# Layer 0's probabilities transposed by DMA, their product with V two steps later, and the queues reordered around it

## The chip, the cores and the metric

The kernel runs on one NeuronCore of a Trainium2 chip. A core has TensorE (PE in the profile, its weight loads as PEld), VectorE (DVE), ScalarE (ACT), GpSimd (POOL), SyncE (SP), which here only issues DMAs, and 16 DMA engines. The metric is the time of one execution on the device in microseconds (us). Each engine runs its own list of instructions in order; they wait for one another through semaphores.

## The reference

Two graph-attention layers over 128 graphs of 128 nodes with 512 channels. What layer 0 computes per graph, with 8 heads of 64 channels:

```python
h = relu(layernorm(x))
m = h @ map_w.T + map_b
n = m_heads / max(norm(m_heads), 1e-8)
cos_adj = ((n @ n.T) * ~mask > 0.1)
q, k = m @ q_w.T + q_b, m @ k_w.T + k_b        # folded into weights that act on h
p = softmax(where(mask, -1e10, q @ k.T / 8))
a = cos_adj * p
x = x + relu((a @ v @ gcn_W.T) / (a.sum(-1) + 1))    # v = h @ gcn_map_w.T + b, gcn_W folded in
```

Layer 1 is a plain masked attention with 4 heads and an output projection on the result. The change leaves it alone.

## The kernel before

Layer 0 takes the graphs in 32 groups of four (QUAD) and walks over 256 **steps**, n = 8 t + u: step u of group t handles graph u // 2 of the group and one half (HB = 4) of its 8 heads. Matrices that need more precision than f16 are split into an f16 high part and an f16 rest, and each product is three f16 matmuls per 128 rows of depth (line 161).

The order of each engine's work is written out by hand in one `group(t)` per engine, without a planner. In step u of group t TensorE runs, in this order: a projection of the next group (m for u < 4, q for u >= 4; 12 matmuls), `prob_transpose(n)` (four f32 transposes through the identity, from `cprobs` in SBUF into the PSUM bank `ps_pt`, line 836), `scores(n + 1)` (8 f32 matmuls of q and k at line 821, 12 f16 matmuls of n with n at line 828, all into the one pair of banks `ps_sc`), a second projection (v or k), and `weigh_values(n)` (12 matmuls of 66 columns into `ps_av`, line 848). So a step needs results of its own step: the transposes wait for `select_similar(n)` on VectorE, `weigh_values(n)` waits for `cpT_low(n)`.

The loop through the other engines is: `row_max` (VectorE, four instructions with mask and row maximum, line 119), `exps` (ScalarE, four exponentials with their sums, line 504), `select_similar` (VectorE, line 620, gives `cprobs`), the transposes on TensorE, `cpT_high` (ScalarE, line 511: PSUM to f16), `cpT_low` (VectorE, line 626: the f16 rest), `row_max` of the next step. `probs` and `cprobs` have one buffer each. After `weigh_values` VectorE runs `epilogue(n)` (three instructions, lines 636 to 644), GpSimd adds the residual (line 422), and SP stores the graph (line 325) and loads the next residual (line 321).

Beside it the next groups are prepared: `stats` (VectorE, lines 84 and 86; all four graphs of a group in step 7), `factors` (GpSimd), `relu` and `h_high` (ScalarE, lines 464 and 470), `h_low` (VectorE, line 582), `transpose_h` (SP, a DMA transpose of 128 x 1024 f16 into `hT`, line 311); and for n: `m_copy` (VectorE, line 587), `square` (ScalarE, line 485), `head_sums` (VectorE), `head_norms` (15 chained GpSimd instructions for each graph) and `normalise` (GpSimd), `n_high` (ScalarE, line 490), `n_low` (VectorE, line 604), `transpose_n` (SP, the same size, line 317). A projection waits until the one before it in its PSUM bank has been copied out (`m_copy`, `v_copy`, `q_copy` line 474, `k_copy` line 479). SP issues every DMA of the kernel from one queue, in program order, waits included; x comes by one DMA of 1 MB for each group.

## Time and profile before

| what | value |
|---|---|
| median of three runs | 2928.79 us (2925.0 to 2929.02) |
| the profiled execution's own time | 2929.56 us |
| its span, first to last instruction | 2927.2 us |
| mean granted TensorE clock | 0.98 |
| busy over the span: PE, DVE, ACT, POOL | 96%, 67%, 59%, 52% |
| DMA moved | 318.36 MB, 109 GB/s on average |

The profile is of one execution. Busy shares are means over stages with different limits: layer 0 runs up to about 1960 us, layer 1 from there on. The end of a matmul is modelled, so the distance from one group's start to the next group's start is what says how long a piece of TensorE's work takes.

### The profile page before, as it was taken

What the parts mean: (1) busy time and instruction counts of PE and PEld (TensorE: products, weight loads), DVE (VectorE), ACT (ScalarE), POOL (GpSimd) and SP (SyncE); (2) the same over time, 40 slices, a digit from 0 to 9 for tenths busy, and PEclk for the clock granted to TensorE, in tenths of its full rate; (3) what the DMA queues carried; (4) which work ended last, traced back from release to release, by engine and by line L of the source; (5) the groups of instructions that cost most, each with busy time, mean ns of one, the idle gap of its engine ahead of it and who ended that gap; (6) DMA issues with size and microseconds to landing.
All of it is one profiled execution on the core that took longest, in us unless ns stands there. A gap on an engine that the chain in (4) does not pass through costs nothing. (4 is left out here: it accounts for less than half of the span.)

```text
span 2927.2 us, 65410 instructions
## 1 busy us (share of the span) xinstructions
PE 2796.1 (96%) x21910; PEld 1596.1 (55%) x21910; DVE 1950.6 (67%) x6356; ACT 1724.5 (59%) x4891; POOL 1531.0 (52%) x4146
## 2 busy tenths in 40 slices
PE   5999999999999999999999999948999999999997
PEld 2455555555555555555555555534555555555554
DVE  4576677667666766676676667656667676666764
ACT  3466556656655665566566556545666666666663
POOL 1565556556645665565566456513455554555441
PEclk8999999999999999999999999969999999999998
DMA  4244334533443443344333434335565555655652
GB/s 128 52 88 110 89 83 94 110 82 88 98 100 82 88 109 97 81 92 114 82 88 96 103 82 88 80 102 123 142 159 153 154 149 144 162 148 157 151 132 65
DMA packets 555741, 318.36 MB, mean 109 GB/s; under 512 B 452496, under 2 KB 454032, under 8 KB 555408
## 3 DMA queue, kind: packets, MB, share of 16 engines
q1 hardware_dynamic: 555408, 314.19, 44.4%
q8 instruction: 176, 2.88, 0.4%
q14 instruction: 157, 1.29, 0.1%
HBM read 146.32 MB, written 67.11 MB: 73 GB/s over the span
## 5 line engine op out<-in xcount | busy, mean ns | idle before, releaser
L504 ACT ACTIVATE probs<-probs,negmax 128x128 f32<-128x128 f32 x1024 | 398.2, 390 | 423.6 <-DVE negmax L119 423.6
L422 POOL TENSOR_TENSOR o_sb<-o_sb,xres 128x512 f32<-128x512 f32 x128 | 162.7, 1271 | 434.6 <-DVE o_sb L644 434.6
L626 DVE SCALAR_TENSOR_TENSOR cpT_lo<-ps_pt,cpT_hi 128x512 f16<-128x512 f32 x256 | 176.7, 690 | 296.3 <-ACT cpT_hi L511 296.3
L161 PE MATMUL ps_pj<-wm_hi,hT 128*128 128x512 f16 x1024 | 326.5, 380 | 15.0 <-DVE wm_lo L669 15.0
L161 PE MATMUL ps_pj<-wv_hi,hT 128*128 128x512 f16 x1024 | 326.8, 380 | 0.0
L161 PE MATMUL ps_pj<-hT,wk_hi 128*128 128x512 f16 x1024 | 305.8, 380 | 0.0
L161 PE MATMUL ps_pj<-hT,wq_hi 128*128 128x512 f16 x1024 | 304.5, 379 | 0.0
L511 ACT ACTIVATE cpT_hi<-ps_pt 128x512 f16<-128x512 f32 x256 | 151.5, 592 | 256.3 <-PE ps_pt L836 256.3
L1102 ACT ACTIVATE l_probs<-l_probs,l_negmax 128x128 f32<-128x128 f32 x512 | 199.1, 390 | 150.2 <-DVE l_negmax L119 150.2
L1071 POOL TENSOR_TENSOR l_xres<-l_xres,l_bo_rows 128x512 f32<-128x512 f32 x128 | 172.9, 1351 | 150.9 <-DMA l_xres<-x_scratch 150.9
L119 DVE CUSTOM_DVE_ANT_0 probs<-ps_sc,mask 128x128 f32<-128x128 f32 x1024 | 233.9, 284 | 3.6 <-PE ps_sc L828 3.6
L836 PE MATMUL ps_pt<-ident,cprobs 128*128 128x128 f32 x1024 | 158.3, 278 | 52.7 <-DVE cprobs L620 52.7
L161 PE MATMUL ps_pj<-wm_lo,hT 128*128 128x512 f16 x512 | 194.7, 380 | 0.0
L161 PE MATMUL ps_pj<-wv_lo,hT 128*128 128x512 f16 x512 | 194.0, 379 | 0.0
L161 PE MATMUL ps_pj<-hT,wq_lo 128*128 128x512 f16 x512 | 194.0, 379 | 0.0
L161 PE MATMUL ps_pj<-hT,wk_lo 128*128 128x512 f16 x512 | 194.0, 379 | 0.0
L620 DVE SCALAR_TENSOR_TENSOR cprobs<-ps_sc,bound,probs 128x512 f32<-128x512 f32 x256 | 189.8, 742 | 4.9 <-ACT probs L504 4.5
L504 ACT ACTIVATION_READ_ACCUMULATOR probs<-probs,negmax 128x1 f32 x1024 | 191.0, 187 | 0.0
L161 PE MATMUL l_ps_pj<-l_wv_hi,l_hT 128*128 128x256 f16 x1024 | 189.8, 274 | 0.0
L836 PEld LDWEIGHTS ps_pt<-ident,cprobs 128*128 128x128 f32 x1024 | 126.5, 143 | 111.2 <-DVE cprobs L620 69.2
L821 PE MATMUL ps_sc<-room 64*128 64x128 f32 x2048 | 186.0, 301 | 0.0
L84 DVE BATCH_NORM_STATS2 ln_st<-xg 128x6 f32<-128x512 f32 x256 | 173.1, 676 | 15.2 <-DMA xg<-in_x 14.9
(196 smaller groups left out, 7204.1 us busy)
## 6 DMA issues: line engine op xcount, KB each, us to landing
xg<-in_x SPq DMA_DIRECT2D x32, 1024.0 KB, 5.6
xres<-in_x SPq DMA_DIRECT2D x128, 256.0 KB, 2.9
x_scratch<-o_sb SPq DMA_DIRECT2D x128, 256.0 KB, 2.1
xg<-x_scratch SPq DMA_DIRECT2D x128, 256.0 KB, 3.0
l_xres<-x_scratch SPq DMA_DIRECT2D x128, 256.0 KB, 3.4
out<-l_o_sb SPq DMA_DIRECT2D x128, 256.0 KB, 3.7
mask_u<-in_adj SPq DMA_DIRECT2D x32, 64.0 KB, 2.8
hT<-h SPq DMA_TRANSPOSE x128, 3.2
```

The source lines that it names most:

```text
L84: nc.vector.bn_stats(st[:, 0:6], x).then_inc(bn_done, 1)
L119: last = nc.vector.tensor_tensor_reduce(masked[:, i], scores[:, i // 2, (i % 2) * P:(i % 2 + 1) * P], mask, -1.0, FLOAT_MAX, ALU.add, ALU. ...
L161: last = pe.matmul(out, a(kt), b(kt), start=(n == 0), stop=(n == 3 * kts - 1))
L422: nc.gpsimd.tensor_tensor(o_sb[:, j % 2], o_sb[:, j % 2], xres[:, j % 2], ALU.add).then_inc(res_done, 1)
L504: last = nc.scalar.activation(probs[:, i], probs[:, i], ACT.Exp, bias=negmax[:, u % 2, i:i + 1], scale=-1.0, accum_out=zsum[:, u % 4, hh:h ...
L511: nc.scalar.activation(cpT_hi[:], ps_pt[:].rearrange("p (h n) -> p h n", h=HB), ACT.Copy, scale=F16_SCALE).then_inc(cph_done, 1)
L620: nc.vector.scalar_tensor_tensor(cprobs[:].rearrange("p (b h) n -> p b (h n)", b=2), ps_c, bound[:, t % 2, j:j + 1], probs[:].rearrange("p ...
L626: nc.vector.scalar_tensor_tensor(cpT_lo[:], ps_pt[:].rearrange("p (h n) -> p h n", h=HB), F16_SCALE, cpT_hi[:], ALU.mult, ALU.subtract).th ...
L821: nc.tensor.matmul(ps_s[:, b, pl * P:(pl + 1) * P], q_sb[rows, t % 2, pr, cols], k_sb[rows, t % 2, pr, cols], start=True, stop=True)
L836: mm = nc.tensor.transpose(ps_pt[:, hh * P:(hh + 1) * P], cprobs[:, hh], ident[:])
L1071: nc.gpsimd.tensor_tensor(xres[:, n % 2], xres[:, n % 2], bo_rows[:], ALU.add).then_inc(res_ready, 1)
L1102: last = nc.scalar.activation(probs[:, hh], probs[:, hh], ACT.Exp, bias=negmax[:, n % 2, hh:hh + 1], scale=-1.0, accum_out=zsum[:, n % 2, ...
```

## The change

- `prob_transpose`, `ps_pt`, `cpT_high` and `cpT_low` go. `p_high` (ScalarE) and `p_low` (VectorE) split `cprobs` where it lies, in SBUF, into `c16` (two buffers of 128 x 1024 f16, both parts), and SP transposes that by DMA into `cpT` (four buffers): one `transpose_p(n)` in each step.
- `weigh_values(n - 2)` and `epilogue(n - 2)` run in step n; the last two steps' follow after the loop. The freed PSUM banks give `ps_sc` and `ps_av` a second buffer each, so `scores(n)` waits for step n - 2 of the readers and no longer for n - 1. The banks of the weights' norms are shared with these.
- x is loaded graph by graph (256 KB each, waiting only for its own graph's `relu`), and `stats` of a group are spread: one graph in steps 5 and 6, two in step 7, all behind the epilogue.
- GpSimd's `head_norms` treats two graphs in one chain of 15 instructions on twice the width, in steps 2 and 4; `n_high`, `n_low` and `transpose_n` come one step later.
- In SP's list the store and the residual load stand behind the step's transposes, and for the graph whose last half was finished by the epilogue of the step before. `add_residual` moves back by one graph accordingly.
- `stage["v"]`, used in the weights' preparation alone, takes the place of half of `hT`.

The core of the diff (changes of names in the preparation are left out):

```diff
-stage["v"] = sb("stage_v", [P, KT, D])[:]
+hT = sb("hT", [P, 2, 2 * KT, QUAD * P], F16)
+stage["v"] = hT[:, 1].rearrange("p k n -> p (k n)").bitcast(F32).rearrange("p (k n) -> p k n", k=KT)
...
-hT = sb("hT", [P, 2, 2 * KT, QUAD * P], F16)
...
-norm_st = sb("norm_st", [P, 2, 4, H0])
-consts = sb("consts", [P, 4, H0])
+norm_st = sb("norm_st", [P, 4, QUAD, H0])
+consts = sb("consts", [P, 4, 2 * H0])
...
-cpT_hi = sb("cpT_hi", [P, HB, P], F16)
-cpT_lo = sb("cpT_lo", [P, HB, P], F16)
+c16 = sb("c16", [P, 2, 2, HB, P], F16)
+cpT = sb("cpT", [P, 4, 2 * HB, P], F16)
...
-ps_sc = ctx.enter_context(nc.psum_tensor("ps_sc", [P, 2, 512], F32))
-ps_s, ps_c = ps_sc[:, :, 0:2 * P], ps_sc[:, :, 2 * P:]
-ps_pt, ps_av = bank("ps_pt"), bank("ps_av")
+ps_sc = [ctx.enter_context(nc.psum_tensor(f"ps_sc{n}", [P, 2, 512], F32)) for n in range(2)]
+ps_s = [both[:, :, 0:2 * P] for both in ps_sc]
+ps_c = [both[:, :, 2 * P:] for both in ps_sc]
+ps_av = [bank("ps_av0"), bank("ps_av1")]
...
-const_loaded, x_loaded = sem("const_loaded"), sem("x_loaded")
+ps_norm = [ps_av[1][:], ps_sc[1][:, 0], ps_sc[1][:, 1], ps_av[0][:]]
+const_loaded = sem("const_loaded")
+x_loaded = [sem(f"x_loaded{j}") for j in range(QUAD)]
...
-pj_ready, s_ready, pt_ready, av_ready = pe_sems = [
-    sem(n) for n in ("pj_ready", "s_ready", "pt_ready", "av_ready")]
+cpT_loaded = [sem(f"cpT_loaded{n}") for n in range(2)]
+pj_ready, s_ready, av_ready = pe_sems = [sem(n) for n in ("pj_ready", "s_ready", "av_ready")]
...
     def load_weight(dst, src, loaded):
...
-    sp.dma_start(xg[:], xt[0]).then_inc(x_loaded, 16)
+    def load_graph(g, j):
+        if g:
+            sp.wait_ge(relu_done, count(QUAD * (g - 1) + j + 1))
+        sp.dma_start(xg[:, j], xrt[g, j]).then_inc(x_loaded[j], 16)
+    for j in range(QUAD):
+        load_graph(0, j)
...
+    def transpose_p(n):
+        sp.wait_ge(cpl_done, count(n + 1))
+        if n >= 4:
+            sp.wait_ge(av_ready, count(n - 3))
+        sp.dma_start_transpose(cpT[:, n % 4], c16[:, n % 2].rearrange("p s h n -> p (s h n)")).then_inc(
+            cpT_loaded[n % 2], 16)
     def load_residual(t, j):
...
-    def load_graphs(g):
-        sp.wait_ge(relu_done, count(QUAD * g))
-        sp.dma_start(xg[:], xt[g]).then_inc(x_loaded, 16)
...
-    sp.dma_start(xg[:], xt[1]).then_inc(x_loaded, 16)
+    for j in range(QUAD):
+        load_graph(1, j)
...
-    load_graphs(2)
+        load_graph(2, j)
...
     def group(t):
...
-            if u % 2 == 0 and t + u:
-                i = QUAD * t + u // 2
-                store(*divmod(i - 1, QUAD))
-                if i + 1 < B:
-                    load_residual(*divmod(i + 1, QUAD))
...
-            if proj and 3 <= u < 3 + QUAD:
-                transpose_n(t + 1, u - 3)
+            if proj and 4 <= u:
+                transpose_n(t + 1, u - 4)
...
-            if t + 3 < GROUPS and u == 6:
-                load_graphs(t + 3)
+            transpose_p(8 * t + u)
+            i = QUAD * t + u // 2 - 2
+            if u % 2 == 0 and i >= 0:
+                store(*divmod(i, QUAD))
+                load_residual(*divmod(i + 2, QUAD))
+            if t + 3 < GROUPS and 3 <= u < 3 + QUAD:
+                load_graph(t + 3, u - 3)
...
+    store(GROUPS - 1, QUAD - 2)
...
     def head_norms(g, j):
...
-        pool.wait_ge(sum_done, count(QUAD * g + j + 1))
-        n2, r, a, vh = (norm_st[:, j % 2, n] for n in range(4))
-        link = chained(pool, norm_chain, count(NORM_OPS * (QUAD * g + j)), NORM_OPS)
+        pool.wait_ge(sum_done, count(QUAD * g + j + 2))
+        n2, r, a, vh = (norm_st[:, n, j:j + 2] for n in range(4))
+        minus_half, three_halves = (consts[:, n].rearrange("p (j h) -> p j h", j=2) for n in range(2))
+        link = chained(pool, norm_chain, count(NORM_OPS * (2 * g + j // 2)), NORM_OPS)
...
-        rsqrt_steps(nc, link, r, n2, vh, a, consts[:, 0], consts[:, 1])
+        rsqrt_steps(nc, link, r, n2, vh, a, minus_half, three_halves)
...
     def normalise(g, j):
...
-        pool.wait_ge(norm_chain, count(NORM_OPS * (QUAD * g + j + 1)))
-        nc.gpsimd.tensor_tensor(heads, heads, norm_st[:, j % 2, 1].unsqueeze(2).to_broadcast([P, H0, DH]),
+        pool.wait_ge(norm_chain, count(NORM_OPS * (2 * g + j // 2 + 1)))
+        nc.gpsimd.tensor_tensor(heads, heads, norm_st[:, 1, j].unsqueeze(2).to_broadcast([P, H0, DH]),
...
     def v_low(g, j):
...
-        normalise(0, j)
+        if j % 2:
...
+            normalise(0, j - 1)
+            normalise(0, j)
...
     def group(t):
...
-                head_norms(t + 1, u - 1)
+            if proj and u in (2, 4):
+                head_norms(t + 1, u - 2)
+                normalise(t + 1, u - 2)
...
-            if u % 2:
-                add_residual(t, u // 2)
+            i = QUAD * t + (u - 3) // 2
+            if u % 2 and i >= 0:
+                add_residual(*divmod(i, QUAD))
...
+    add_residual(GROUPS - 1, QUAD - 1)
...
 def _(act):
...
-    def cpT_high(n):
-        act.wait_ge(pt_ready, count(n + 1))
-        act.wait_ge(av_ready, count(n))
-        nc.scalar.activation(cpT_hi[:], ps_pt[:].rearrange("p (h n) -> p h n", h=HB), ACT.Copy,
-                             scale=F16_SCALE).then_inc(cph_done, 1)
+    def p_high(n):
+        act.wait_ge(cp_done, count(n + 1))
+        act.wait_ge(cpT_loaded[n % 2], 16 * (n // 2))
+        nc.scalar.activation(c16[:, n % 2, 0], cprobs[:], ACT.Copy, scale=F16_SCALE).then_inc(cph_done, 1)
...
     def weight_high(n, kind):
...
+            p_high(n)
...
-            cpT_high(n)
...
-            if proj and 2 <= u < 2 + QUAD:
-                n_high(t + 1, u - 2)
+            if proj and 3 <= u < 3 + QUAD:
+                n_high(t + 1, u - 3)
...
     def stats(g, j):
-        dve.wait_ge(x_loaded, 16 * (g + 1))
+        dve.wait_ge(x_loaded[j], 16 * (g + 1))
...
     def head_sums(g, j):
...
-        dve.wait_ge(n_done, count(QUAD * g + j - 1))
-        nc.vector.tensor_reduce(norm_st[:, j % 2, 0], sq[:].rearrange("p (h c) -> p h c", h=H0), AX_X,
+        if g:
+            dve.wait_ge(n_done, count(QUAD * (g - 1) + j + 1))
+        nc.vector.tensor_reduce(norm_st[:, 0, j], sq[:].rearrange("p (h c) -> p h c", h=H0), AX_X,
...
     def n_low(g, j):
...
-        mask_scores(nc, dve, s_ready, count(n + 1), probs, ps_s, mask[:, t % 2, u // 2],
+        mask_scores(nc, dve, s_ready, count(n + 1), probs, ps_s[n % 2], mask[:, t % 2, u // 2],
...
     def select_similar(n):
...
-        dve.wait_ge(pt_ready, count(n))
-        nc.vector.scalar_tensor_tensor(cprobs[:].rearrange("p (b h) n -> p b (h n)", b=2), ps_c,
+        nc.vector.scalar_tensor_tensor(cprobs[:].rearrange("p (b h) n -> p b (h n)", b=2), ps_c[n % 2],
...
-    def cpT_low(n):
+    def p_low(n):
...
-        nc.vector.scalar_tensor_tensor(cpT_lo[:], ps_pt[:].rearrange("p (h n) -> p h n", h=HB), F16_SCALE,
-                                       cpT_hi[:], ALU.mult, ALU.subtract).then_inc(cpl_done, 1)
+        nc.vector.scalar_tensor_tensor(c16[:, n % 2, 1], cprobs[:], F16_SCALE, c16[:, n % 2, 0], ALU.mult,
+                                       ALU.subtract).then_inc(cpl_done, 1)
...
     def epilogue(n):
...
-        av = ps_av[:].rearrange("p (h n) -> p h n", h=HB)
+        av = ps_av[n % 2][:].rearrange("p (h n) -> p h n", h=HB)
...
-            if proj and 3 <= u < 3 + QUAD:
-                n_low(t + 1, u - 3)
-            cpT_low(n)
+            if proj and 4 <= u:
+                n_low(t + 1, u - 4)
+            p_low(n)
...
-            if t + 3 < GROUPS and u == 7:
-                for j in range(QUAD):
-                    stats(t + 3, j)
...
-            epilogue(n)
+            if n >= 2:
+                epilogue(n - 2)
+            if t + 3 < GROUPS and u > QUAD:
+                stats(t + 3, u - QUAD - 1)
+                if u == 7:
+                    stats(t + 3, QUAD - 1)
...
+    epilogue(8 * GROUPS - 2)
+    epilogue(8 * GROUPS - 1)
...
 def _(pe):
...
-        pe.wait_ge(negmax_done, count(n))
-        pe.wait_ge(cp_done, count(n))
+        pe.wait_ge(negmax_done, count(n - 1))
+        pe.wait_ge(cp_done, count(n - 1))
...
-                nc.tensor.matmul(ps_s[:, b, pl * P:(pl + 1) * P], q_sb[rows, t % 2, pr, cols], k_sb[rows, t % 2, pr, cols],
+                nc.tensor.matmul(ps_s[n % 2][:, b, pl * P:(pl + 1) * P], q_sb[rows, t % 2, pr, cols], k_sb[rows, t % 2, pr, cols],
...
-                    mm = nc.tensor.matmul(ps_c[:, b, pl * P:(pl + 1) * P], nT[rows, t % 2, j, KT * x_part + pr],
+                    mm = nc.tensor.matmul(ps_c[n % 2][:, b, pl * P:(pl + 1) * P], nT[rows, t % 2, j, KT * x_part + pr],
...
-    def prob_transpose(n):
-        pe.wait_ge(cp_done, count(n + 1))
-        pe.wait_ge(cpl_done, count(n))
-        for hh in range(HB):
-            mm = nc.tensor.transpose(ps_pt[:, hh * P:(hh + 1) * P], cprobs[:, hh], ident[:])
-        mm.then_inc(pt_ready, 1)
...
     def weigh_values(n):
...
-        pe.wait_ge(cpl_done, count(n + 1))
-        pe.wait_ge(epi_chain, count(EPI_OPS * n))
+        pe.wait_ge(cpT_loaded[n % 2], 16 * (n // 2 + 1))
+        pe.wait_ge(epi_chain, count(EPI_OPS * (n - 1)) if n else BASE)
...
-            for i, (probs_part, v_part) in enumerate(((cpT_hi, v_hi), (cpT_hi, v_lo), (cpT_lo, v_hi))):
-                mm = nc.tensor.matmul(ps_av[:, hh * P:hh * P + VW], probs_part[:, slot(hh)],
+            for i, (probs_part, v_part) in enumerate(((0, v_hi), (0, v_lo), (1, v_hi))):
+                mm = nc.tensor.matmul(ps_av[n % 2][:, hh * P:hh * P + VW], cpT[:, n % 4, HB * probs_part + slot(hh)],
...
-            prob_transpose(n)
...
-            weigh_values(n)
+            if n >= 2:
+                weigh_values(n - 2)
...
+    weigh_values(8 * GROUPS - 2)
+    weigh_values(8 * GROUPS - 1)
...
```

## Rows read from the trace of the kernel before

**Rows 1.** Windows: length, busy PE, PEld, DVE, ACT, POOL, clock, DMA share, GB/s

```profile
117.70:1909.10 1791.40, 1760.38 (x14882) 990.09 (x14880) 1232.42 (x4086) 1078.80 (x3099) 1037.29 (x2803) 1.00 0.40 92
...
1041.47:1099.01 57.54, 56.79 (x481) 31.95 (x480) 39.92 (x132) 34.94 (x100) 33.65 (x91) 1.00 0.37 93
```

**Rows 2.** Timeline of PE over one step: start, length in us, what

```profile
1006.12 0.60 PE L836 MATMUL ps_pt<-ident,cprobs 128*128 128x128 f32 x4
1006.65 0.71 PE L821 MATMUL ps_sc<-room 64*128 64x128 f32 x8
...
1007.63 0.39 PE L161 MATMUL ps_pj<-wv_hi,hT 128*128 128x512 f16 x1
...
1010.60 0.38 PE L161 MATMUL ps_pj<-wm_hi,hT 128*128 128x512 f16 x1
...
1013.19 0.60 PE L836 MATMUL ps_pt<-ident,cprobs 128*128 128x128 f32 x4
```

**Rows 3.** Waits, 146 to 1870 us: us in total, times, longest

```profile
PE ps_pt L836 <- DVE cprobs L620: 26.0, 29, 1.7
```

**Rows 4.** Groups by line and form: busy us, mean ns, idle before

```profile
L626 DVE SCALAR_TENSOR_TENSOR cpT_lo<-ps_pt,cpT_hi 128x512 f16<-128x512 f32 x256 | 176.7, 690 | 296.3 <-ACT cpT_hi L511 296.3
...
L511 ACT ACTIVATE cpT_hi<-ps_pt 128x512 f16<-128x512 f32 x256 | 151.5, 592 | 256.3 <-PE ps_pt L836 256.3
...
L604 DVE SCALAR_TENSOR_TENSOR n<-m_sb,n 128x512 f16<-128x512 f32 x128 | 101.5, 793 | 12.1 <-ACT n L490 12.1
```

**Rows 5.** Timeline of DVE across a group's boundary

```profile
1044.67 0.69 DVE L84 BATCH_NORM_STATS2 ln_st<-xg 128x6 f32<-128x512 f32 x1 [0.17 <-DMA xg<-in_x]
...
1047.88 0.18 DVE L636 SCALAR_TENSOR_TENSOR epi_st<-zsum,v_den,ps_av 128x4 f32<-128x4 f32 x1
...
1048.66 0.74 DVE L620 SCALAR_TENSOR_TENSOR cprobs<-ps_sc,bound,probs 128x512 f32<-128x512 f32 x1
...
1051.39 0.28 DVE L119 CUSTOM_DVE_ANT_0 probs<-ps_sc,mask 128x128 f32<-128x128 f32 x1
...
1052.23 0.75 DVE L587 SCALAR_TENSOR_TENSOR m_sb<-ps_pj,w_st,mb 128x512 f32<-128x512 f32 x1
```

**Rows 6.** Timeline of ACT in a loaded step

```profile
1030.40 0.40 ACT L504 ACTIVATE probs<-probs,negmax 128x128 f32<-128x128 f32 x1 [1.60 <-DVE negmax L119]
...
1031.95 0.76 ACT L479 ACTIVATE room<-ps_pj,kb,w_st 128x512 f32<-128x512 f32 x1
...
1033.15 0.80 ACT L464 ACTIVATE h<-xg,ln_st 128x512 f32<-128x512 f32 x1
...
1034.60 0.78 ACT L474 ACTIVATE room<-ps_pj,qb,w_st 128x512 f32<-128x512 f32 x1
...
1060.97 0.61 ACT L485 ACTIVATE sq<-m_sb 128x512 f32<-128x512 f32 x1
```

**Rows 7.** Timeline of SP's queue, a burst of DMA transposes

```profile
1026.22 1.24 SPq L317 DMA_TRANSPOSE space<-n  x1
...
1030.29 1.35 SPq L311 DMA_TRANSPOSE hT<-h  x1
```

**Rows 8.** Windows of half a us: behind that burst, and in a load

```profile
1032.50:1033.00 0.50, 0.50 (x4) 0.26 (x3) 0.50 (x2) 0.50 (x2) 0.08 (x1) 1.00 0.02 2
...
1042.00:1042.50 0.50, 0.50 (x9) 0.50 (x10) 0.00 (x0) 0.50 (x2) 0.00 (x0) 1.00 1.05 410
```

**Rows 9.** DMA issues: count, KB each, median us to landing

```profile
hT<-h SPq DMA_TRANSPOSE x128, 3.2
```

**Rows 10.** Timeline of PE in the last group, two steps

```profile
1934.87 1.12 PE L836 MATMUL ps_pt<-ident,cprobs 128*128 128x128 f32 x4 [2.83 <-DVE cprobs L620]
...
1941.39 1.11 PE L836 MATMUL ps_pt<-ident,cprobs 128*128 128x128 f32 x4 [2.83 <-DVE cprobs L620]
```

**Rows 11.** Timeline of SP's queue, layer 1's first DMA

```profile
1963.02 0.93 SPq L1000 DMA_DIRECT2D l_mask_u<-in_adj  x2
```

**Rows 12.** Timeline of SP's queue, the first issue

```profile
0.74 0.46 SPq L292 DMA_DIRECT2D xg<-in_x  x1
```

More of the change, by code:

```diff
@@ L683, in _ @@
             dve.wait_ge(norm_ready, 1)
-            weight_scale(0, ps_norm[0][:])
+            weight_scale(0, ps_norm[0])
             weight_low(0, "q")
             dve.wait_ge(norm_ready, 2)
-            weight_scale(1, ps_norm[1][:])
+            weight_scale(1, ps_norm[1])
             dve.wait_ge(prep_stage, 3 * KT)
@@ L711, in _ @@
             dve.wait_ge(norm_ready, 4)
-            weight_scale(3, ps_av[:])
+            weight_scale(3, ps_norm[3])
             weight_low(3, "m")
@@ L858, in _ @@
                 if n == KT + 2:
-                    norms(0, ps_norm[0][:])
+                    norms(0, ps_norm[0])
                 if n == 0:
@@ L879, in _ @@
                 mm.then_inc(prep_mm, 1)
-            norms(1, ps_norm[1][:])
+            norms(1, ps_norm[1])
             pe.wait_ge(prep_bias, 1 + 2 * KT)
@@ L883, in _ @@
                 cols = slice((n % KT) * P, (n % KT + 1) * P)
-                mm = nc.tensor.matmul(ps_s[:, 0, n:n + 1], bias_rows[:, n // KT, cols], ones_col[:], start=True, stop=True)
+                mm = nc.tensor.matmul(ps_sc[0][:, 0, n:n + 1], bias_rows[:, n // KT, cols], ones_col[:], start=True, stop=True)
             mm.then_inc(prep_mm, 1)
             for pr in range(PAIRS0):
-                mm = nc.tensor.matmul(ps_sc[:, 1, pr * P:(pr + 1) * P], gb_rows[:, pr, :], gw_bd, start=True, stop=True)
+                mm = nc.tensor.matmul(ps_sc[0][:, 1, pr * P:(pr + 1) * P], gb_rows[:, pr, :], gw_bd, start=True, stop=True)
             mm.then_inc(prep_mm, 1)
-            norms(2, ps_pt[:])
-            norms(3, ps_av[:])
+            norms(2, ps_norm[2])
+            norms(3, ps_norm[3])
             pe.wait_ge(prep_lo, 4)
```

12 lines of the change are left out of this document (5 added, 7 removed).

## The prediction

> **What bounds the kernel now.** I read the windows first. From 117.70 us, where step 0 of group 0 begins on TensorE, to 1909.10 us, where step 0 of the last group begins, 31 groups take 1791.4 us, and TensorE is busy for 1760.4 of them. VectorE is busy for 69%, ScalarE for 60%, GpSimd for 58%, the DMA engines for 40% [rows 1]. One group from the middle takes 57.54 us [rows 1]. Then the timeline of TensorE: a step has no gap. From one transpose to the next it is 1013.19 - 1006.12 = 7.07 us: transposes 0.53, scores 0.98, second projection and the product with V 2.97, first projection 2.59 [rows 2]. So in layer 0 the end is set by TensorE's own work. Eight such steps are 56.56 us, and a group has 0.98 us more. The waits name most of that: TensorE waits for `cprobs` 29 times, once per group, 0.9 us each [rows 3], in step 0, where VectorE comes late because four `stats` stand in its step 7 [rows 5]. In sum, 1791.4 - 248 x 7.07 = 38.0 us are not dense steps. In the last group nothing is projected, and the loop through all engines sets the pace: 1941.39 - 1934.87 = 6.52 us per step [rows 10]. Layer 1 begins at 1963.02 [rows 11], 53.9 us after 1909.10. The granted clock is 1.00 in the 31 groups [rows 1].
>
> **The transposes leave TensorE.** 0.53 us in each of the 248 steps with projections is 131.4 us, all on the path, since the steps are dense. The step becomes 7.07 - 0.53 = 6.54 us and a group 52.32, if nobody else is slower. Nothing else of TensorE's work changes; the two products with V that are missing in steps 0 and 1 come back after the loop.
>
> **The stall in step 0.** TensorE no longer needs `cprobs` of its own step. `scores(n + 1)` wants the readers of step n - 1, the product with V wants data two steps old. What TensorE still needs soon is `m_copy`, for the next projection. I follow VectorE from the product with V that ends step 7: about 0.2 until it is seen, epilogue 0.78, two `stats` at 0.80 (four of them took 1047.88 - 1044.67), `select_similar` 0.74, then `p_high` on ScalarE 0.60, `p_low` 0.69, `row_max` 0.84, `m_copy` 0.75 [rows 4, 5]. That is 6.2 us of the 6.54, so it fits with 0.3 to spare. `p_low` has two SBUF inputs where `cpT_low` had one, like `n_low`, which takes 793 ns on average against 690 [rows 4]: I take 0.1 us more for it and 0.2 us of stall per group, bounds 0 and the 0.98 of before. In group 0 four `stats` (3.2 us) stay in step 0: VectorE's work there is 0.74 + 0.60 (waiting for `p_high`) + 0.69 + 0.84 + 0.75 + 3.2 + about 0.75 (`v_copy`) = 7.6, so some 1.3 us late. The 38.0 become 31 x 0.2 + 1.3 = 7.5: 30.5 us saved.
>
> **The loop through VectorE and ScalarE.** `probs` has one buffer, so the loop `exps`, `select_similar`, `p_high`, `p_low`, `row_max` stays. In-order lists put other work into it. From `exps` in step 3 to `exps` in step 4: `exps` 1.55, `n_high` about 0.54 (it and `k_copy` take 1.20 together), `relu` and `h_high` 1.45, `square` 0.61 and `v_high` as much, `p_high` 0.60, `p_low` 0.69, `row_max` 0.84, handovers 0.15: 7.04 us [rows 4 to 6]. That is 0.5 more than a step. The neighbours are shorter: from step 4 to 5 `k_copy` comes in and `square`, `v_high` go, 6.5; from 6 to 7 `relu` and `h_high` go too, about 5. ScalarE's whole list in step 4 is 1.22 + 0.60 + 0.68 (`q_copy`) + 1.55 + 1.20 + 1.45 = 6.7. The lateness reaches TensorE only through `q_copy`, which has 2 us of slack in step 4, or through `scores`, which has a whole step. I cost it at nothing; with the cover gone it is 0.7 us per group (the 0.5 and ScalarE's 0.2), 22 us.
>
> **GpSimd.** One norm chain for two graphs instead of two spares it two chains of 15 instructions per group. `n_high` of graph 0 comes one step later, and by my count `normalise` is ready 0.7 us before it. Costed at nothing, since GpSimd is busy for 58% [rows 1].
>
> **SP and the DMA engines.** Eight more transposes per group, each as large as `transpose_h`. In the burst of four, the first is issued at 1026.22 and the fourth at 1030.29, 1.36 us apart [rows 7], and at 1032.50 the engines are silent [rows 8]: (1032.50 - 1026.22) / 4 = 1.57 us each is the upper bound of that burst. One alone lands 3.2 us after its issue [rows 9]. The bounds are thus 1.36 and 3.2, and I take 1.36, since the new transposes stand in the same queue behind the same neighbours. A copy of 256 KB at 410 GB/s [rows 8] is 0.64 us. Per group: 16 x 1.36 + 12 x 0.64 = 29.5 us of 52.5. The fullest steps are 4 to 6, with three transposes (n, h, p) and up to three copies: 4.1 + 1.9 = 6.0 us, still under 6.54; SP's issue time is 3 x 1.36 + 3 x 0.46 = 5.5 [rows 7, 12]. Two waits hang on it. `p_high(n)` wants `transpose_p(n - 2)` landed, because `c16` has two buffers: `p_low(n - 2)` ends about 4.4 us into its step, behind it come up to three issues and 3.2 us to landing, so about 11 us, and `p_high(n)` starts at 13.1 + 2. The product with V wants it at 19. Both hold. The store and the residual load wait for an `add_residual` that is some 5 us old by then, so what is queued behind them (the x load, the next step's transposes) is not held up; this takes away the long waits at the store that held the queue before.
>
> The Trainium skill ("VectorE: DVE Perf Modes", The three transpose paths, and its rules for authors) speaks against this change: a 128 x 128 transpose should go to TensorE where PSUM will do, and by DMA it takes 1309 ns against 390. Estimated from that figure alone, eight blocks one by one would be 10.5 us per instruction, longer than any step, and layer 0 would be about three times as long. The trace bounds a whole instruction of eight blocks at 1.57 us in a burst, so it does not agree with using the page's figure as a rate.
>
> **The last group.** The loop without TensorE in it: 0.74 + 0.60 + 0.69 + 0.84 + 1.55 + handovers 0.15 = 4.57 against 6.52, over seven intervals 13.7 us less. At the end the last transpose has to land (3.2) and one product and one epilogue are left over (0.6 + 0.78): 4.6 more. Net 9 us saved, bounds 0 (the weights of layer 1 are in the same queue and delay `transpose_p`) and 13.
>
> **Before the loop.** Four x issues where there was one put the weights 3 x 0.46 = 1.4 us later [rows 12]: 1.4 lost, at least 0.
>
> **Sum.** 2929.56 - 131.4 - 30.5 - 9 + 1.4 = 2760 us. The profiled execution is 0.8 us above the median of the runs, which does not matter here. Layer 1 is not touched.
>
> **Rivals.**
> - *Loop and group boundary bind (0.13).* For it: 7.04 us in one step and 6.7 us of ScalarE in another, 0.3 us of slack at `m_copy`, 0.7 at `n_high`, all worked out. Against: each is one step of eight, and TensorE has slack behind it. It would cost 0.7 per group, and with the old 0.98 of stall instead of 0.2 together 1.5: 2760 + 22 to 46 = 2782 to 2806.
> - *The queue binds in part (0.06).* From 2.4 us per transpose, steps 4 to 6 leave a backlog of 3 x (7.2 + 1.9 - 6.54) = 7.7 us, the slack of the product with V. At 2.9, a group needs 16 x 2.9 + 7.7 = 54.1: 2810.
> - *Slower: the DMA transposes do not overlap (0.03).* If each holds the engines from issue to landing, 3.2 us, a group needs 16 x 3.2 + 7.7 = 58.9 us, 6.4 more than 52.5: 2760 + 198 = 2958. It decides from about 3.15 us each (52.5 + 170 / 31 = 58.0 per group). Against it stands the burst of rows 7 and 8; for it, that no stretch of the trace holds more than a few transposes in a row. The page's rule above ends on this side.
> - *The time is not given back (0.02).* TensorE's list gets shorter, but the steps stay at 7.07 because another engine paces them: about 2929. VectorE is the nearest, 39.92 us of 57.54 [rows 1] and 0.8 more by `p_low`, 78% of 52.5.
>
> **The numbers.** My forecast has 0.76. Its own range: 7.5 less if no stall is left and 4 less with the best last group, 18 more with half of the stall left and nothing gained in the last group: 2748 to 2778. To reach 8 in 10 the range takes in the first rival: 2742 to 2806. 0.2%, about 6 us, is what a measurement of this kernel can tell from no change. Faster: 0.76 + 0.13 + 0.06 = 0.95; within 0.02; slower 0.03.
>
> **What would show it.** Steps of 6.54 us on TensorE and groups of 52.3 to 52.6; no transposes at line 836; next to no TensorE wait for `m_sb`; transposes of `c16` issued 1.3 us apart and landing in 3 to 6 us; ScalarE not waiting for the DMA of `cpT`; steps of about 4.6 us in the last group. I would be wrong if TensorE waits for a DMA of `cpT` or ScalarE for it (the queue), if TensorE waits for `m_sb` or `room` in every group by over 0.5 us (the loop), or if the granted clock falls below 1.00 in the 31 groups.

## The result, and the profile after

The changed kernel takes 2785.27 us (median of four runs, 2783.91 to 2790.43) against 2928.90 beside it on the same chip. The ratio is 0.9512, with a 95% interval of 0.9497 to 0.9526: 143.6 us faster. The forecast was 2760 with a range of 2742 to 2806, so the direction and the range held and the size was 25 us too good. My forecast's own range, 2748 to 2778, was missed: 2785 lies in the part of the range that I had added for the first rival, and that rival is not what happened (see below).

The profiled execution, the slowest of the four, took 2790.43 us with a span of 2787.1, against 2929.56 and 2927.2 before. I divide both spans at the same four places: the first scores of TensorE, the scores of step 248 (the first of the last group), the first DMA of layer 1, and the end. In this table "stalls" are the 248 intervals of the 31 groups less 248 dense steps. They are 3.0 us less than the 38.0 of the prediction, before and after alike, because the prediction divided at other places: its stretch starts behind the first scores and ends behind step 247, so it holds one more second projection and product with V (2.97 us).

| stretch, us | before | after | saved | forecast |
|---|---|---|---|---|
| to the first scores | 116.70 | 121.71 | -5.0 | -1.4 |
| 248 dense steps | 248 x 7.07 = 1753.4 | 248 x 6.634 = 1645.2 | 108.1 | 131.4 |
| stalls in the 31 groups | 1788.4 - 1753.4 = 35.0 | 1651.1 - 1645.2 = 5.9 | 29.1 | 30.5 |
| last group, to layer 1's first DMA | 57.9 | 53.9 | 4.0 | 9 |
| layer 1 | 964.2 | 960.4 | 3.8 | 0 |
| sum | 2927.2 | 2787.1 | 140.1 | 169.5 |

The windows of the changed kernel, the 31 groups and one group from the middle, with the columns of [rows 1]:

```profile
121.71:1772.80 1651.09, 1644.74 (x13842) 866.88 (x13841) 1281.90 (x4072) 1070.53 (x3092) 877.26 (x1872) 1.00 0.68 139
1084.73:1137.80 53.07, 53.07 (x450) 28.00 (x449) 40.61 (x131) 34.67 (x100) 28.52 (x61) 1.00 0.70 136
```

TensorE is busy from end to end, the clock is 1.00, VectorE is at 78% and the DMA engines are at 0.68 of their time where they were at 0.40. In the dense steps TensorE still sets the pace, so there the sum can only be off in TensorE's own work. Its timeline over one step, which answers to [rows 2]:

```profile
991.55 0.38 PE L161 MATMUL ps_pj<-wm_hi,hT 128*128 128x512 f16 x1
991.86 0.71 PE L843 MATMUL ps_sc<-room 64*128 64x128 f32 x8
...
992.84 0.39 PE L161 MATMUL ps_pj<-wv_hi,hT 128*128 128x512 f16 x1
...
995.81 0.38 PE L161 MATMUL ps_pj<-wm_hi,hT 128*128 128x512 f16 x1
...
998.49 0.71 PE L843 MATMUL ps_sc<-room 64*128 64x128 f32 x8
```

The step is 998.49 - 991.86 = 6.63 us and not 6.54. The scores take 0.98 as before, the second projection with the product with V 2.97 as before. The first projection takes 998.49 - 995.81 = 2.68 where it took 2.59: its last matmul starts at 991.55, the scores 0.31 later, while one matmul follows another there every 0.215 us. The missing 0.09 us sits at the entry into the scores. Weight loads on the same stretch name it:

```profile
991.33 0.10 PEld L161 LDWEIGHTS ps_pj<-wm_hi,hT 128*128 128x128 f16 x1
991.86 0.52 PEld L843 LDWEIGHTS ps_sc<-room 64*128 64x128 f32 x8 [0.42 <-issue]
...
992.84 0.10 PEld L161 LDWEIGHTS ps_pj<-wv_hi,hT 128*128 128x128 f16 x1
```

The weights of a projection are loaded 0.22 us before their matmul starts (991.33 for 991.55). The first 64-row weights start to load only when their matmul does. (Behind the scores the first 128-row weights, too, load only at 992.84, when their matmul starts; before the change the same two pieces stood there, so this is no part of the missing 0.09.)

What is left of the stall is in the waits between 200 and 1750 us (us in total, times, longest), and in the timelines of VectorE and of SP's queue at the one place where it is long:

```profile
DVE ln_st L84 <- DMA xg<-in_x: 7.2, 10, 2.8
...
PE ps_pj L161 <- DVE m_sb L605: 4.3, 5, 2.5
```

```profile
1136.84 0.18 DVE L86 BATCH_NORM_AGGREGATE ln_st<-ln_st 128x2 f32<-128x6 f32 x1
1139.79 0.69 DVE L84 BATCH_NORM_STATS2 ln_st<-xg 128x6 f32<-128x512 f32 x1 [2.77 <-DMA xg<-in_x]
1140.52 0.18 DVE L86 BATCH_NORM_AGGREGATE ln_st<-ln_st 128x2 f32<-128x6 f32 x1
1140.62 0.72 DVE L638 SCALAR_TENSOR_TENSOR cprobs<-ps_sc,bound,probs 128x512 f32<-128x512 f32 x1
```

```profile
1132.60 0.45 SPq L296 DMA_DIRECT2D xg<-in_x  x1
1133.15 1.24 SPq L324 DMA_TRANSPOSE space<-n  x1
1134.49 9.49 SPq L330 DMA_TRANSPOSE cpT<-c  x2
```

(The last line holds two issues and SP's wait between them.) The `stats` of the fourth graph stand in VectorE's step 7, its x is issued less than a step earlier, and here it landed 7.2 us after its issue. VectorE waits in order, so `select_similar`, `p_low` and `m_copy` come late, and TensorE with them. In the other nine late steps TensorE is late by 0.14 to 0.15 us less than VectorE waited for x. In this one VectorE waited for 2.77 us and the step is 4.16 us too long, because something came on top (the second line has the columns of [rows 1]):

```profile
1144.38 0.59 PE L161 MATMUL ps_pj<-wm_hi,hT 128*128 128x512 f16 x1 [2.46 <-DVE m_sb L605]
```

```profile
1144.38:1148.60 4.22, 4.22 (x13) 1.46 (x13) 2.87 (x6) 2.52 (x9) 2.23 (x7) 0.63 0.62 168
```

After an idle of 2.46 us the granted clock was 0.63 on average until the next scores, part of the stretch at the lower of its two levels (1.2 GHz), and the first projection took 4.22 us instead of 2.68. So of the 7.3 us in ten late steps, 1.5 are the clock's.

### The profile page after: what moved, and what is told of

It is laid out like the page before. It is cut to its first block and busy times, and to the rows that moved or that the text cites. A ratio compares the mean times of both kernels' runs of the same rounds, so it can differ in the third digit from the quotient of the medians.

```text
span 2787.1 us, 62486 instructions
## 1 busy us (share of the span) xinstructions
PE 2678.5 (96%) x20883; PEld 1472.3 (53%) x20886; DVE 2006.2 (72%) x6356; ACT 1717.9 (62%) x4891; POOL 1365.4 (49%) x3186
## 5 line engine op out<-in xcount | busy, mean ns | idle before, releaser
L644 DVE SCALAR_TENSOR_TENSOR c<-cprobs,c 128x512 f16<-128x512 f32 x256 | 182.9, 714 | 82.2 <-ACT c L530 81.9
L530 ACT ACTIVATE c<-cprobs 128x512 f16<-128x512 f32 x256 | 160.3, 626 | 120.0 <-DVE cprobs L638 115.3
L600 DVE TENSOR_TENSOR h<-h 128x512 f16<-128x512 f32 x128 | 109.9, 859 | 130.1 <-ACT h L489 130.1
L843 PEld LDWEIGHTS ps_sc<-room 64*128 64x128 f32 x2048 | 136.3, 189 | 115.2 <-issue 115.1
L429 POOL TENSOR_TENSOR v_lo<-v,v_hi 128x512 f16<-128x512 f32 x128 | 168.7, 1318 | 28.2 <-ACT v_hi L514 25.1
```

The lines of the kernel that those rows point to most:

```text
L429: nc.gpsimd.tensor_tensor(dst, v32[:, j % 2].rearrange("p (h c) -> p h c", h=H0), high, ALU.subtract).then_inc(vlo_done, 1)
L530: nc.scalar.activation(c16[:, n % 2, 0], cprobs[:], ACT.Copy, scale=F16_SCALE).then_inc(cph_done, 1)
L600: nc.vector.tensor_tensor(h16[:, j % 2, D:], h32[:, j % 2], h16[:, j % 2, 0:D], ALU.subtract).then_inc(hlo_done, 1)
L644: nc.vector.scalar_tensor_tensor(c16[:, n % 2, 1], cprobs[:], F16_SCALE, c16[:, n % 2, 0], ALU.mult, ALU.subtract).then_inc(cpl_done, 1)
L843: nc.tensor.matmul(ps_s[n % 2][:, b, pl * P:(pl + 1) * P], q_sb[rows, t % 2, pr, cols], k_sb[rows, t % 2, pr, cols], start=True, stop=True)
```

## Experiments

In the table, "first" is the start of the first scores, "dense" the usual step, "excess" what the 30 groups after the first take above dense steps (in so many of 240 steps), "tail" the stretch from the scores of step 248 to layer 1's first DMA; all from the timeline of TensorE. Layer 1 took 958.9 to 964.2 us in these fourteen profiles, and both ends are profiles of the same kernel, the one before.

| kernel | first | dense | excess | tail | span |
|---|---|---|---|---|---|
| before | 116.7 | 7.07 | 32.5 (29) | 57.9 | 2927.2 |
| before, again | 118.7 | 7.07 | 31.3 (29) | 57.1 | 2921.8 |
| before, x by graph and spread stats | 120.8 | 7.07 | 30.6 (85) | 58.5 | 2927.6 |
| after | 121.7 | 6.63 | 7.3 (10) | 53.9 | 2787.1 |
| after, again | 120.3 | 6.63 | 7.6 (11) | 52.7 | 2786.8 |
| dummy transposes | 120.9 | 7.07 | 0.0 (0) | 53.8 | 2886.3 |
| f16 products first | 122.0 | 6.60 | 12.4 (16) | 52.8 | 2784.1 |
| all stats in step 7 | 120.6 | 6.63 | 38.7 (29) | 53.0 | 2815.1 |
| weights first | 119.9 | 6.63 | 10.4 (18) | 54.0 | 2790.4 |
| AV one step behind | 120.1 | 6.63 | 7.8 (9) | 54.6 | 2789.9 |
| double transposes | 120.2 | 6.63 | 61.5 (31) | 54.9 | 2841.8 |
| layer 1's loads early | 120.7 | 6.63 | 11.8 (14) | 50.5 | 2787.9 |
| fourth stats later | 122.0 | 6.63 | 0.0 (0) | 52.5 | 2779.0 |
| four edits together | 118.2 | 6.60 | 0.0 (0) | 50.4 | 2764.3 |

**What are four transposes worth?** The changed kernel with four of them in each step again:

```diff
 def scores(n):
...
+    for hh in range(HB):
+        nc.tensor.transpose(ps_s[n % 2][:, hh // 2, (hh % 2) * P:(hh % 2 + 1) * P], ident[:], ident[:])
```

> The changed kernel with four f32 transposes of ident put back ahead of the scores of each step, behind the wait for room, their result overwritten by the scores. Output unchanged. Theory (0.10 of the 0.53 us is the entry from 128-row work into the 64-row f32 score tiles, which stays; the four transposes are 0.43): the dense step goes from 6.63 to 7.06 to 7.07 us, the whole by 256 x 0.43 = 110 us. Rival (the transposes are worth the whole 0.53 and the missing 0.09 is another instruction that became longer): 7.16 us, the whole by 136 us.

The dense step is 7.07, so four transposes are worth 0.44 us and not 0.53. The whole grew by 99 us instead of 110, mostly because the 7.3 us of excess went at the same time (with steps of 7.07 VectorE is never late there), and 1.3 us of TensorE's waits in group 0 with them. Its timelines of TensorE's matmuls and of its weight loads:

```profile
994.14 0.38 PE L161 MATMUL ps_pj<-wm_hi,hT 128*128 128x512 f16 x1
994.36 0.60 PE L840 MATMUL ps_sc<-ident 128*128 128x128 f32 x4
994.89 0.71 PE L845 MATMUL ps_sc<-room 64*128 64x128 f32 x8
```

```profile
993.93 0.10 PEld L161 LDWEIGHTS ps_pj<-wm_hi,hT 128*128 128x128 f16 x1
994.14 0.57 PEld L840 LDWEIGHTS ps_sc<-ident 128*128 128x128 f32 x4
994.88 0.29 PEld L845 LDWEIGHTS ps_sc<-room 64*128 64x128 f32 x3 [0.17 <-issue]
```

The transposes with 128-row weights are entered 0.22 us after the last projection matmul, their first weights loaded ahead, although they stand behind the semaphore waits. The 64-row scores come 0.53 later with weights loaded late again. So of the 0.53 between the first transpose and the first scores, which I read from [rows 2] as the price of the transposes, 0.09 is the entry into the 64-row tiles, and it stays when the transposes go.

**Is it the type or the tile?** The f16 products go ahead of the f32 ones:

```diff
 def scores(n):
...
-            nc.tensor.matmul(ps_s[n % 2][:, b, pl * P:(pl + 1) * P], q_sb[rows, t % 2, pr, cols], k_sb[rows, t % 2, pr, cols],
-                             start=True, stop=True)
...
                     nc.tensor.matmul(ps_c[n % 2][:, b, pl * P:(pl + 1) * P], nT[rows, t % 2, j, KT * x_part + pr],
...
+            mm = nc.tensor.matmul(ps_s[n % 2][:, b, pl * P:(pl + 1) * P], q_sb[rows, t % 2, pr, cols], k_sb[rows, t % 2, pr, cols],
+                                  start=True, stop=True)
     mm.then_inc(s_ready, 1)
```

> The changed kernel with the f16 products of the similarity ahead of the f32 products of the scores in each step. Theory (the first 64-row tile after 128-row tiles is loaded only when the work before it has drained, whatever its type): the step stays at 6.63 us within 0.02, with the same gap of about 0.1 us at the first weight load of the f16 products. Rival (it is the f32 load that is not made ahead): the gap sits at the change from f16 to f32, or goes; the step changes by 0.05 to 0.1 us, 12 to 25 us in all.

```profile
991.48 0.10 PEld L161 LDWEIGHTS ps_pj<-wm_hi,hT 128*128 128x128 f16 x1
992.00 0.34 PEld L844 LDWEIGHTS ps_sc<-space 64*128 64x128 f16 x12 [0.42 <-issue]
992.30 0.52 PEld L850 LDWEIGHTS ps_sc<-room 64*128 64x128 f32 x8
```

The same [0.42 <-issue] stands ahead of f16 weights now, and the f32 ones behind them are loaded ahead. So it is not the type. That it is the 64 rows, and not something else that these tiles share, was not tried apart. The step is 6.60, 0.04 less than without this edit and outside the 0.02 that I allowed; the entry still takes 0.31 us, and the two kinds of products behind it 0.95 instead of 0.98; why this order is shorter I did not follow up. A dense group takes 52.76 us instead of 53.07, 9.3 us over 30 groups, but the excess is 5.1 us more than in the changed kernel: 4 us came out. VectorE has less time in a shorter step, which fits, but the excess of five profiles with steps of 6.63 and the same `stats` already lies between 7.3 and 11.8 us, so one profile does not show it.

The Trainium skill ("TensorE: Matmul & The Clock Gate", The mechanism) says that a weight load is pulled ahead of running matmuls when it goes to another row group or to the background weight buffer, and a few lines on that it overlaps only when the row group differs. These traces agree with the first sentence for full tiles and not with the second, since 128-row loads overlap with 128-row matmuls; for the change from 128 to 64 rows they show no overlap.

**The stall at the group's boundary: where the stats stand.** First, the changed kernel with all four in step 7, behind the epilogue:

```diff
-if t + 3 < GROUPS and u > QUAD:
-    stats(t + 3, u - QUAD - 1)
-    if u == 7:
-        stats(t + 3, QUAD - 1)
+if t + 3 < GROUPS and u == 7:
+    for j in range(QUAD):
+        stats(t + 3, j)
```

> The changed kernel with all four stats of VectorE in step 7 again, behind the epilogue, as before the change, and the rest as changed. Theory (the spreading is what removed the stall of each group boundary): 4 x 0.80 us less the two that stand there already puts m_copy 1.6 us later, of which 0.1 to 0.3 us was free: TensorE waits for m_sb in each of 27 groups by 1.3 to 1.6 us, 35 to 43 us in all. Rival (the stall went because TensorE no longer waits for cprobs, the spreading gives nothing): under 5 us.

```profile
PE ps_pj L161 <- DVE m_sb L605: 32.8, 28, 1.2
```

One step of each group takes 7.96 instead of 6.63, 1.33 us late for 1.6 us of stats. That leaves 0.27 us of slack with two of them; the prediction had counted 0.3 by hand. The theory holds in so far as the new order of TensorE without the spreading leaves as large a stall as before the change, 38.7 us. Second, the kernel before with x by graph and the stats spread, nothing else:

```diff
-if t + 3 < GROUPS and u == 7:
-    for j in range(QUAD):
-        stats(t + 3, j)
...
 epilogue(n)
+if t + 3 < GROUPS and u > QUAD:
+    stats(t + 3, u - QUAD - 1)
+    if u == 7:
+        stats(t + 3, QUAD - 1)
```

> The kernel before with two parts of the change alone: x by graph, and the stats of VectorE spread over steps 5, 6 and 7 instead of all in step 7. The transposes stay on TensorE. Theory (the stall of each boundary is the four stats in a row): the wait for cprobs in step 0, 0.9 us in 29 groups, goes: 25 to 30 us faster, 2900 us. Rival (with the product with V in the same step something else is just as late): under 5 us.

This theory fell: the excess is 30.6 against 31.3 and 32.5 (25.6 of it in step 0, the rest 0.09 us at a time behind the one stats of step 5 and of step 6). VectorE at the boundary in this run:

```profile
1219.72 0.22 DVE L640 SCALAR_TENSOR_TENSOR epi_st<-zsum,v_den,ps_av 128x4 f32<-128x4 f32 x1 [1.74 <-PE ps_av L853]
...
1220.52 0.68 DVE L84 BATCH_NORM_STATS2 ln_st<-xg 128x6 f32<-128x512 f32 x1
...
1221.34 0.66 DVE L84 BATCH_NORM_STATS2 ln_st<-xg 128x6 f32<-128x512 f32 x1
...
1222.13 0.74 DVE L624 SCALAR_TENSOR_TENSOR cprobs<-ps_sc,bound,probs 128x512 f32<-128x512 f32 x1
```

TensorE wants `cprobs` when its first projection is done, 2.59 us [rows 2] after the product with V that the epilogue waited for. From the start of the epilogue to the end of `select_similar` it is 1222.87 - 1219.72 = 3.15. The step is 7.95 there, and with one stats (steps 5 and 6) it is 7.16. Before the change the four stats stood ahead of the epilogue [rows 5], partly inside a wait for the product with V that is 1.74 us long here; two behind it cost 0.88 us, four ahead of it 1.1 on average (32.5 / 29). So neither part removes the steady stall alone: the spreading in the old order leaves 30.6 us, the new order without the spreading 38.7, both together none in most groups. In steps of 7.07 us the spreading would be needed too: by estimate four stats would still come 1.6 - 0.27 - 0.44 = 0.9 us late in each group (the two stats more, less the slack and less the longer step). A spread ahead of the epilogue was not tried.

**What is left of the stall.** The fourth graph's stats go one step later:

```diff
 if t + 3 < GROUPS and u > QUAD:
     stats(t + 3, u - QUAD - 1)
-    if u == 7:
-        stats(t + 3, QUAD - 1)
+if t and ahead and u == 0:
+    stats(t + 2, QUAD - 1)
```

> The changed kernel with one edit: the stats of the fourth graph move from VectorE's step 7 to step 0 of the next group, behind the epilogue. Theory (what is left of the boundary stall, 6 us in 9 of the 31 groups of the changed kernel, is VectorE waiting in order for the fourth graph's x, which landed up to 7 us after its issue): VectorE's waits for x in layer 0 fall from 8.9 us to under 1, every group but the first takes 53.07 us within 0.1, 5 to 6 us faster. Rival (another wait stands behind it, the stats make step 1 late or GpSimd's factors come late): groups over 53.3 us stay, or come in every group.

```profile
121.98:1765.75 1643.77, 1641.84 (x13842) 865.86 (x13841) 1285.71 (x4072) 1073.04 (x3092) 872.30 (x1872) 1.00 0.68 139
```

No step of the 30 groups is over the dense one by as much as 0.05 us, and the 31 groups take 1643.8 us instead of 1651.1: 7.3 us, a little more than expected. VectorE's wait for x no longer appears between 200 and 1750 us, although the fourth graph's x still took up to 7.0 us from issue to landing. The rival, GpSimd's factors coming late, cost nothing.

**How much room does the DMA queue have?** Every `c16` is transposed a second time into a spare buffer, 24 instead of 16 transposes per group:

```diff
 def transpose_p(n):
...
+    sp.wait_ge(spare_loaded, 16 * n)
+    sp.dma_start_transpose(spare[:], c16[:, n % 2].rearrange("p s h n -> p (s h n)")).then_inc(spare_loaded, 16)
```

> The changed kernel with a second transpose of every c16 into a spare buffer that nobody reads: 24 instead of 16 DMA transposes per group. Output unchanged. Theory (1.36 us each in the queue, with room left in all): a group needs 24 x 1.36 + 7.7 = 40 us of 53.4, but steps 4 to 6 get 4 x 1.36 + 1.9 = 7.3 us against 6.63, a backlog of 2 us that the two steps of slack cover: at most 1 us per group, under 30 us in all. Rival (each costs 2 us or more when they come steadily): 24 x 2 + 7.7 = 55.7 us per group, 70 us or more in all.

```profile
120.20:1825.45 1705.25, 1654.79 (x13842) 869.05 (x13841) 1287.49 (x4072) 1070.36 (x3092) 875.82 (x1872) 0.99 0.89 172
```

```profile
DVE ln_st L84 <- DMA xg<-in_x: 54.6, 28, 3.4
...
PE ps_pj L161 <- DVE m_sb L610: 46.2, 28, 3.1
```

The 31 groups take 54.2 us more, between what the two theories gave, and the place is neither's. TensorE never waits for `cpT` between 200 and 1750 us, ScalarE waits three times for the spare transposes (2.5 us in all), and the dense step stays at 6.63. The lateness comes out in one step per group, at the fourth graph's stats: the same wait as in the changed kernel, 54.6 instead of 7.2 us. But it is not a slower transfer. SP issues that x 10.2 us after the start of `scores(8 t + 7)` instead of 8.1, because the second transposes stand ahead of it, and from issue to landing it takes 4.2 us in both kernels (medians of 29 groups). What grew is the time until the issue. In five of the 31 late steps, behind idle times of 2.1 to 3.1 us, the granted clock fell as in the changed kernel's long one, and the first projection took 1.4 to 1.7 us more: 7.9 us of the 61.5. Behind an idle of 2.9 us in another of them it did not. The windows also price a transpose for the DMA engines: (0.89 x 1705.25 - 0.68 x 1651.09) / 248 = 1.59 us, and from [rows 1] to after (1122.7 - 716.6) / 248 = 1.64.

**Two steps behind, or one?**

```diff
-if n >= 2:
-    weigh_values(n - 2)
+if n >= 1:
+    weigh_values(n - 1)
```

(the epilogue likewise)

> The changed kernel with the product with V and the epilogue one step behind the scores instead of two. Theory (p_low ends some 4.4 us into its step, the transpose lands 3.2 to 6 us later, and the product with V stands some 12.7 us after the step's start): no TensorE wait for cpT in most steps, time within 5 us of the changed kernel, 1 us less behind the loop. Rival (the queue is tight in steps 4 to 6, where three transposes and up to three copies are due): TensorE waits for the DMA of cpT in those steps, 1 to 3 us per group, 30 to 90 us in all.

```profile
PEld ps_av L862 <- DMA cpT<-c: 0.6, 2, 0.5
```

In the 30 groups nothing changes, 7.8 us of excess against 7.3. TensorE's weight loads waited for `cpT` twice in 1550 us, 0.6 us together. One step would do there; the tail got longer, because a transpose behind layer 1's loads now holds TensorE for 9.4 us instead of 6.0.

**The last group.** Layer 1's x and weights are loaded in step 1 of the last group but one:

```diff
-if not proj and u == 2:
+if t == GROUPS - 2 and u == 1:
...
-    sp.wait_ge(s_ready, count(8 * (GROUPS - 1)))
```

> The changed kernel with the loads of layer 1's x and weights issued in step 1 of the last group but one, where SP has room, instead of step 2 of the last group. Theory (the last group's one gap of 8.66 us is transpose_p(250) standing behind these loads): that gap becomes 4.7 us and the kernel 4 us faster. Rival (the gap is from something else at the same place): it stays at 8.66.

In the changed kernel TensorE waits once for 6 us (step of 8.66), and SP's queue shows for what:

```profile
1800.62 0.23 PE L863 MATMUL ps_av<-v_hi,cpT 128*128 128x66 f16 x1 [6.02 <-DMA cpT<-c]
```

```profile
1785.96 1.95 SPq L361 DMA_DIRECT2D xg<-x_scratch  x4
1787.95 0.43 SPq L365 DMA_DIRECT2D room<-in_wq  x1
...
1790.29 5.88 SPq L330 DMA_TRANSPOSE cpT<-c  x1
```

With the loads early, that step is 4.70 like its neighbours and the tail is 50.5 us instead of 53.9 and 52.7: 2.2 to 3.4 us and not 4. The theory holds for the gap. The span did not show it, since the 30 groups of that run had 4.5 us more of the irregular excess.

**Before the loop.**

```diff
-for j in range(QUAD):
-    load_graph(0, j)
 load_weight(raw_map, map_w, map_loaded)
 load_weight(raw_q, q_wT, q_loaded)
+for j in range(QUAD):
+    load_graph(0, j)
```

> The changed kernel with map_w and the q weights issued ahead of the four x graphs of group 0, at the very start. Theory 1 (the late first weights are what the prologue lost): the first weight transposes of TensorE start at 11.9 us or earlier instead of 13.6, the first scores 1.7 us earlier: 1.7 us gained in all. Theory 2 (the lost clock of the prologue hangs on the order of the loads too): the first scores at about 116.7 as before the change, 5 us gained. Rival (x later means the norms later): nothing gained.

> The kernel before, unchanged, once more. The first scores stood at 116.70 us in its one profile and at 119.9 to 122.0 in eight profiles of kernels that load x by graph. If that difference belongs to the load of x (theory), they stand at 116.7 within 1 us again and the granted clock in the 16 small transposes behind the 3.16 us idle is 1.00; if it is chance of the execution (rival), they stand near 120 and the clock is at 0.50 there.

TensorE starts at 9.80 instead of 13.62, and the first scores stand at 119.9, 1.1 us under the mean of the ten profiles with x by graph ahead of the weights (120.9): less than the first theory's 1.7, and nothing of the second's 5. The ten spread over 2.0 us (120.1 to 122.0), so 1.1 is no firm number; but the combined version below, with the weights first as well, has 118.2, and both lie below all ten. The second profile of the kernel before has the first scores at 118.73, between the 116.7 of the theory and the 120 of the rival. Its first matmul starts within 0.05 us of the first profile's. The two differ most at one place, behind the same idle of 3.16 us (before, then again):

```profile
47.54 2.05 PE L878 MATMUL ps_pj<-room 128*128 128x128 f32 x16 [3.16 <-ACT stage_v L523]
```

```profile
48.16 3.58 PE L878 MATMUL ps_pj<-room 128*128 128x128 f32 x16 [3.16 <-ACT stage_v L523]
```

Sixteen matmuls of 128 columns (products with gcn_W; I had called them transposes) take 2.05 us in the first, where the granted clock is 1.00, and 3.58 in the second, where it is 0.55. The other 0.6 us lie ahead of them. The window of the changed kernel that holds them has a granted clock of 0.50, the lower of the two levels (1.2 GHz):

```profile
49.20:53.20 4.00, 3.78 (x16) 3.66 (x18) 1.94 (x1) 1.22 (x3) 0.00 (x0) 0.50 0.02 4
```

In all twelve other profiles the sixteen take 3.48 to 3.79 us, so the first profile is the exception. So 2.0 of the 5.0 us lost before the loop (118.73 - 116.70) belong to the execution and not to the change, as the rival had it. Against the second profile the ten with x by graph are 2.2 us later on average. That is the price of the four x issues as far as one profile on the other side can tell; TensorE's first matmul starts 1.7 us later (13.62 against 11.90 and 11.95).

**Together.** The last runs hold four of these edits at once, and the changed kernel beside it:

> The changed kernel with four edits together: the f16 products ahead of the f32 ones, the first weights ahead of x, layer 1's loads one group earlier, the fourth graph's stats in step 0 of the next group. If they add up: 248 x 0.035 = 8.7 us from the order of the products, 5 to 6 from the stats, 3.4 from the last group, 1 from the prologue: 19 us under the changed kernel, 2766 us. Rival (the step of 6.60 stays but VectorE has no slack left at the boundary, so that the order gives nothing): 2775 us.

> The changed kernel, unchanged, once more, beside the combined one: 2785 us within 5, the first scores at 120 to 122 us, groups of 53.07 us with some longer ones, 5 to 10 us of them in all, and VectorE's waits for x about 9 us.

The version with the four edits takes 2765.61 us (four runs, 2763.97 to 2766.73), a ratio to the kernel before of 0.9440 with an interval of 0.9424 to 0.9455. The changed kernel on the same chip takes 2786.96 (2782.84 to 2791.24), 0.9514 with 0.9497 to 0.9531. The two intervals do not overlap: 21.4 us more, where 19 were expected. By stretch against the changed kernel beside it: 2.2 before the loop, 17.1 in the 31 groups, 2.3 in the last one, 1.0 in layer 1.

## Why the forecast held, and where it was 25 us off

Luck has a part in the range. My own range ended at 2778, and the forecast of 2760 is off on one side: in the profiled execution 29.4 us are missing (169.5 - 140.1), 23.3 in the first point below, 1.4 in the second, 5.0 in the last group and 3.6 before the loop, less 3.8 in layer 1 that nothing in the change explains.

- **The transposes leave TensorE: the failing term.** I took the 0.53 us from the first transpose to the first scores in [rows 2] as their cost. The dummy transposes show that they are worth 0.44; 0.09 is the late load of the first 64-row weights, which then follows the projection instead. 248 x 0.094 = 23.3 us, most of the miss. That TensorE paces the dense steps was right: TensorE is busy for 53.07 us of 53.07.
- **The stall in step 0.** 29.1 us came of 30.5. The slack was right within 0.03 us (0.27 against 0.3). But what is left is not what I had forecast 7.5 for (8.9 in the prediction's count, 38.0 - 29.1): there is no 0.2 us in each group, and 7.3 us in ten steps come from a wait that I did not name, VectorE's for the fourth graph's x, with 1.5 us of lower clock behind the longest. In group 0 TensorE waits for `m_sb` twice, 1.06 and 0.88 us, where I had one lateness of 1.3. The new order did not remove the stall by itself: without the spreading it is 38.7 us.
- **The loop through VectorE and ScalarE.** Costed at nothing, and nothing is what it shows: steps 3 to 6 are 6.63 like the others. The first rival, 22 to 46 us from this loop and from a stall in every group, did not occur; that the result lies in its stretch of the range is a coincidence.
- **GpSimd.** Costed at nothing as well: in the 31 groups no wait of another engine is put down to it.
- **SP and the DMA engines.** `c16` and the product with V never wait in the 31 groups, as forecast, and landing stays at 3.2 us in the median. The price of 1.36 us per transpose was too low: the engines are busy for 1.6 us by the shares of the windows, a group holds 0.68 x 53.07 = 36 us of DMA time and not 29.5. The late one is the x load that stands between the transposes. The rivals "does not overlap" and "not given back" are refuted. The queue did bind in part, though at another place and for less than the second rival had it. One of my signs of being wrong also came, in a small way: the granted clock fell once, for one step.
- **The price in the Trainium skill.** The Trainium skill ("VectorE: DVE Perf Modes", The three transpose paths) gives a DMA transpose of one 128 x 128 tile 1309 ns. By this trace, eight such blocks in one instruction take 1.6 us of DMA time, so the figure is not a rate here. Its advice to transpose on TensorE does not fit a kernel whose TensorE is full and whose DMA engines are not.
- **The last group.** 4.0 us of 9. The steps are 4.70 against 4.57 worked out. From scores to scores, the seven intervals of the last group took 43.8 us before and 32.7 after: 11.1 less and not 13.7. I had taken 6.52 for each, but only the last three are that long (43.8 is 1.8 less than seven times 6.52), and after the change the gap behind layer 1's loads, which I had named as the bound of 0, made one interval 8.66; it cost 2.2 to 3.4 by the run without it. Behind the last scores 7.1 us more pass than before, where I had 4.6; there TensorE waits for `cpT` three times.
- **Before the loop.** 5.0 instead of 1.4, of which 2.0 are chance of the execution; the four issues cost about 2.2 where 1.4 was forecast, with the caveat above, and the rest lies within the spread of the ten profiles.
- **Layer 1.** 3.8 us less, without an edit there. The kernel before varies by 5.3 us between its own two profiles, so I count it as chance.

## What to carry to other kernels

Price an instruction that you remove by a run with and without it, or at least by what would follow its neighbour: the gap to the next start also holds what the next instruction costs to enter, and that stays. When a wait goes away, ask which in-order engine has a DMA wait just ahead of its critical work; there a queue's lateness came out first here, before anyone waited long for the transfers that were added; look whether the late load was issued late or landed late. Two parts of a change can each be needed and do nothing alone, so take out either one before you say which of them worked. Moving such a consumer by one step cost nothing and gave 7 us, and with it a shorter step on TensorE paid in full.
